# Message sums over edges: one float32 product against two float32r products of a rounded part and the rest

## The reference, cut to what matters

```python
hs = xs @ w_in2f_s / math.sqrt(B)
hv = jnp.einsum('nbc,bf->nfc', xv, w_in2f_v) / math.sqrt(B)
s = hs[idx_j]
v = hv[idx_j]
...
edge = jnp.concatenate([(t_s1 * Wf[..., 0])[..., None], (t_s2 * Wf[..., 1])[..., None],
                        t_v1 * Wf[..., 2:3], t_v2 * Wf[..., 3:4], ...], axis=-1)
agg = jax.ops.segment_sum(edge.reshape(edge.shape[0], -1), idx_i, num_segments=n).reshape(n, F, 16)
s_in = jnp.concatenate([agg[..., 0], agg[..., 1]], axis=1)
v_in = jnp.concatenate([agg[..., 2:5], agg[..., 5:8]], axis=1)
```

## Time and profile before

| | |
|---|---|
| median of 3 runs | 2253.58 us (2251.02 to 2253.9) |
| the profiled execution, own time | 2249.59 us |
| its span | 2247.9 us |
| mean granted clock of PE | 0.991 |
| instructions in the trace | 36380 |

### The profile page before, as it was taken

The page is one execution under the profiler, slowest core; times in us unless marked ns, Lnnn a source line. Parts: engine busy times, 40 slices in busy tenths (PEclk is TensorE's granted clock), DMA queues, the critical chain, the costliest instruction groups (busy, mean ns, idle before and its releaser), DMA issues.

```text
span 2247.9 us, 36380 instructions
## 1 busy us (share of the span) xinstructions
PE 2199.6 (98%) x12269; PEld 1888.6 (84%) x12269; DVE 1487.8 (66%) x4615; ACT 1024.2 (46%) x2028; POOL 937.4 (42%) x931
## 2 busy tenths in 40 slices
PE   8999999979999999999999999999999999999997
PEld 6878878858899888888999999988888777888785
DVE  8777878744767856666326666267776777678675
ACT  5982112222366632222224656344434666676454
POOL 2017637745222234376552223013444554753542
PEclk9999999989999999999999999999999999999998
DMA  6434665443476748787225667356667777776442
GB/s 215 148 133 136 161 194 193 150 137 106 138 249 216 275 151 278 254 285 252 84 92 175 221 225 258 108 187 227 218 219 236 252 251 246 246 256 227 164 124 69
DMA packets 192495, 435.82 MB, mean 194 GB/s; under 512 B 45751, under 2 KB 74622, under 8 KB 191774
## 3 DMA queue, kind: packets, MB, share of 16 engines
q1 hardware_dynamic: 127034, 249.08, 32.2%
q0 software_dynamic: 65296, 184.67, 26.3%
HBM read 242.68 MB, written 190.96 MB: 193 GB/s over the span
## 4 chain that ended last, share of the span: by engine, by line
PE 72%; DVE 2%; DMA 1%; ACT 1%; issue 1%; POOL 0%; POOLq 0%; SPq 0%; ACTq 0%; DVEq 0%
PE g_h_ps L2625 7%; PE g_h_ps L2642 7%; PE g_h_ps L2627 7%; PE g_h_ps L2626 7%; PE g_h_ps L2643 6%; PE g_h_ps L2644 6%; PE g_h_ps L2667 6%; PE g_h_ps L2669 5%; PE g_h_ps L2668 5%; PE g_t_ps L80 4%; PE g_h_ps L1783 2%; PE g_h_ps L1785 2%; PE g_h_ps L1784 2%; PE g_sum_ps L1023 1%; PE g_sum_ps L1022 1%
## 5 line engine op out<-in xcount | busy, mean ns | idle before, releaser
L2764 ACT ACTIVATE g_act_t<-g_t_ps,g_b_col 128x256 f32<-128x256 f32 (+1 forms) x488 | 202.0, 466 | 371.9 <-PE g_t_ps L80 371.7
L2642 PE MATMUL g_h_ps<-g_x_hi,held_w_hi 128*128 128x256 f32 x1216 | 352.5, 290 | 0.0
L2643 PE MATMUL g_h_ps<-g_x_lo,held_w_hi 128*128 128x256 f32 x1216 | 344.2, 283 | 0.0
L2644 PE MATMUL g_h_ps<-g_x_hi,held_w_lo 128*128 128x256 f32 x1216 | 344.1, 283 | 0.0
L632 DVE CUSTOM_DVE_ANT_0 g_prod<-g_h_sb,g_a_rows 128x256 f32<-128x256 f32 x632 | 224.3, 419 | 79.7 <-ACT g_h_sb L513 71.9
L2667 PE MATMUL g_h_ps<-fc_w_hi,g_x_hi 128*128 128x512 f32 x632 | 268.8, 425 | 2.1 <-DVE g_x_lo L2943 2.1
L2625 PE MATMUL g_h_ps<-held_w_hi,g_x_hi 128*128 128x512 f32 x656 | 264.0, 402 | 0.0
L2627 PE MATMUL g_h_ps<-held_w_hi,g_x_lo 128*128 128x512 f32 x656 | 257.2, 392 | 0.0
L2626 PE MATMUL g_h_ps<-held_w_lo,g_x_hi 128*128 128x512 f32 x656 | 257.1, 392 | 0.0
L2669 PE MATMUL g_h_ps<-fc_w_hi,g_x_lo 128*128 128x512 f32 x632 | 247.5, 392 | 0.0
L2668 PE MATMUL g_h_ps<-fc_w_lo,g_x_hi 128*128 128x512 f32 x632 | 247.0, 391 | 0.0
(11 more groups left out here) (401 smaller groups left out, 4834.2 us busy)
## 6 DMA issues: line engine op xcount, KB each, us to landing
h<-g_h_sb SPq DMA_DIRECT2D x120, 512.0 KB, 3.6
h<-g_rows_own SPq DMA_DIRECT2D x40, 512.0 KB, 4.8
g_x_in<-in_dram SPq DMA_DIRECT2D x39, 512.0 KB, 3.9
h_cols<-g_h_sb SPq DMA_DIRECT2D x38, 512.0 KB, 4.9
xb_rows<-in_dram SPq DMA_DIRECT2D x19, 1024.0 KB, 6.1
xb<-xb_rows SPq DMA_DIRECT2D x19, 1024.0 KB, 4.4
g_x_in<-h_cols SPq DMA_DIRECT2D x38, 512.0 KB, 7.6
g_x_in<-h SPq DMA_DIRECT2D x21, 512.0 KB, 6.4
```

Source lines behind the costliest of these rows:

```text
L2642: pe.matmul(out, wh, xh, start=(k == 0), stop=False)
L2643: pe.matmul(out, wh, xl, start=False, stop=False)
L2644: last = pe.matmul(out, wl, xh, start=False, stop=(k == KC - 1))
```

## The change

`sum_edges` no longer makes one float32 product. ACT copies the messages into `msg_hi`, held in float32r, right behind the carry (`carry`, now also called for tile 0, where it makes the copy alone). DVE gets a function `rest`, first in part 1, that forms `msg_lo` = `pmsg` - `msg_hi`. PE makes two products with the same mask, `msg_hi` and `msg_lo`, into one sum. The count of `msg_done` is 4 per tile instead of 3; PE waits for all 4, the others for the first 3 as before.

```diff
+    MSG_STEPS = 4
...
-                pool.wait_ge(self.msg_done, 3 * (t - 3))
+                pool.wait_ge(self.msg_done, self.MSG_STEPS * (t - 4) + 3)
...
     def sum_edges(self, pe, t):
         h = self.hold
         pe.wait_ge(self.masks_done, t + 1)
-        pe.wait_ge(self.msg_done, 3 * t + 3)
+        pe.wait_ge(self.msg_done, self.MSG_STEPS * t + 4)
         if t:
 
-            pe.wait_ge(self.carried, t)
             pe.wait_ge(self.sums_out, t)
-        pe.matmul(h.psum_ps, h.mask[:, t * P:(t + 1) * P].bitcast(F32), h.pmsg[:, :], start=True, stop=True).then_inc(self.summed, 1)
+        mask = h.mask[:, t * P:(t + 1) * P]
+        pe.matmul(h.psum_ps, mask, h.msg_hi[:, :], start=True, stop=False)
+        pe.matmul(h.psum_ps, mask, h.msg_lo[:, :], start=False, stop=True).then_inc(self.summed, 1)
...
-            act.wait_ge(self.msg_done, 3 * t)
+            act.wait_ge(self.msg_done, self.MSG_STEPS * (t - 1) + 3)
...
     def carry(self, act, t):
 
         h = self.hold
-        act.wait_ge(self.msg_done, 3 * t + 3)
-        act.activation(h.pmsg[0:1, :], h.psum_ps[0:1, :], ACT.Copy).then_inc(self.carried, 1)
+        act.wait_ge(self.msg_done, self.MSG_STEPS * t + 3)
+        if t:
+            act.activation(h.pmsg[0:1, :], h.psum_ps[0:1, :], ACT.Copy).then_inc(self.carried, 1)
+            act.wait_ge(self.carried, 2 * t)
+        act.activation(h.msg_hi[:, :], h.pmsg[:, :], ACT.Copy).then_inc(self.carried, 1)
...
+    def rest(self, dve, t):
+        h = self.hold
+        dve.wait_ge(self.carried, 2 * t + 1)
+        dve.tensor_tensor(h.msg_lo[:, :], h.pmsg[:, :], h.msg_hi[:, :].bitcast(F32), ALU.subtract).then_inc(self.msg_done, 1)
...
+        p.msg_hi, p.msg_lo = mid("msg_hi", [P, 10 * F], F32R), mid("msg_lo", [P, 10 * F], F32R)
...
-                        if 0 < n + 1 < ET:
+                        if 0 <= n + 1 < ET:
                             painn.carry(act, n + 1)
...
                     if part == 1:
+                        if 0 <= n + 1 < ET:
+                            painn.rest(dve, n + 1)
                         if 0 <= n - 2 < ET:
                             painn.add(dve, n - 2)
```

## The result

| | before | after |
|---|---|---|
| median | 2252.3 us (4 runs, 2250.44 to 2253.9) | 2270.02 us (4 runs, 2268.39 to 2272.79) |
| ratio of the times | | 1.0081, 95% interval 1.0067 to 1.0095 |
| span of the profiled execution | 2247.9 us | 2268.0 us |
| mean granted clock of PE | 0.991 | 0.988 |

The change makes the kernel 17.7 us slower.

What follows compares the result with a forecast made beforehand. PE was taken to bound the kernel. Waits of 11.7 + 3.7 + 0.85 - 0.4 = 15.9 us less 5.0 saved gave 10.9 us slower, 2264.5 us on the median; range 2254 to 2271.

Steps and rivals of the forecast that it cites:

- What bounds, and where the loss arises: PE bounds the stretch; it waits for the rest, which stands behind DVE's node-layer work, in 11 tiles, 11.7 us.
- The range: Predicted times for the whole kernel from 2254 to 2271 us, around a forecast of 2264.5 us.
- C: Rival at the edge sum on PE: two float32r products cost as much as one float32 product, 2269.5 us; 8%.
- D: Rival: ACT and DVE queues push into eight even tiles too, 6.9 us more, 2271.4 us; 12%.
- The waits: PE's waits ahead of msg_hi's product in tile 0 and the odd tiles, 15.9 us net with ACT's share and second-order terms.
- ACT's push on the shift: The copy ahead of the root on ACT delays DVE's shift 0.46 us in eight odd tiles, 3.7 us.
- The wait for the transfer: PE's existing 0.39 us wait in tile 1, which a later PE no longer sees: -0.4 us.
- Paid anew each time: DVE's lateness recurs in each odd tile, since the even tile's add between waits for PE's product.
- B: Rival: PE's wait is paid once, only the longest counting, 2.6 us in tile 19; 2251.2 us; 10%.
- The saving: Two float32r products replace PE's float32 edge sum, 0.29 us for 0.54, saving 0.25 us per tile, 5.0 us.
- rule on weight loads: Loads overlap running products only for another row group, about 107 ns each; by it 0.04 us saved per tile.
- so a late product delays them one for one: Node-layer products behind the edge sum on PE start later by exactly the wait's length, with nothing extra.

## Why the prediction was right, and where it fell short

- **What bounds, and where the loss arises**: right. PE is the bound, and PE waits in tile 0 and in the odd tiles for a rest that stands behind the node layer's work. A version that moves only that instruction takes the loss away, and so does one that leaves it out.
- **The range**: in part luck. 2270.02 us is 5.5 above the forecast of 2264.5 and 1 below the top of the range. The range reached so high for C (2269.5) and a part of D (2271.4), and the forecast's own spread ended at 2270; neither C nor D took place, and the loss of clock had no part in it. The time by itself would have spoken for C or D. Only the steps of the tiles tell them apart.
- **The waits**: right in the nine odd tiles from 3 on, a little small. The forecast steps of the nine odd tiles from 3 to 19 sum to 12.3 us, measured 13.6 (table), each 0.03 to 0.23 us more. The signal from DVE to PE takes 0.09 us, not 0.05; the copy takes 0.47 us, not 0.44; ACT's push on the shift is (8.7 - 4.7) / 8 = 0.50 us, not 0.46. Tile 8 was called tight and wasn't (-0.30 us for a forecast of -0.11). Tile 1 had a wait that the forecast lacked: the rest on DVE ended at 1925.68 us there and PE's product started at 1925.78, after 0.40 us of idle time. The wait for the transfer was gone, as forecast, so that the step came out at -0.21 us, not -0.65.
- **Paid anew each time**: right. Every odd tile waits in both profiles of the changed kernel, so B falls; no even tile but tile 0 waits, so D falls.
- **The saving**: its size was right, 0.26 us per tile by the even steps against 0.25, 5.3 us in all; its parts were not. These are tile 14 before and, without a wait, tile 14 of the changed kernel:

```profile
2014.58 0.49 PE L1534 MATMUL g_h_ps<-painn_o2s,painn_scal 128*128 128x128 f32 x2
2014.91 0.70 PE L1496 MATMUL g_sum_ps<-painn_msg,g_mask 128*128 128x320 f32 x2
...
2015.68 0.40 PE L2668 MATMUL g_h_ps<-fc_w_lo,g_x_hi 128*128 128x512 f32 x1
...
2028.63 0.49 PE L1536 MATMUL g_h_ps<-painn_o2s,painn_scal 128*128 128x128 f32 x2
2028.87 0.39 PE L1497 MATMUL g_sum_ps<-painn_msg_hi,g_mask 128*128 128x320 f32 x1
2029.10 0.30 PE L1498 MATMUL g_sum_ps<-painn_msg_lo,g_mask 128*128 128x320 f32 x1
2029.25 0.39 PE L2678 MATMUL g_h_ps<-fc_w_hi,g_x_hi 128*128 128x512 f32 x1
2029.47 0.40 PE L2679 MATMUL g_h_ps<-fc_w_lo,g_x_hi 128*128 128x512 f32 x1
```

  From the last product of `out_two` to the second one of the node layer it is 1.10 us before and 0.84 with the change. But the two products start 0.23 us apart, not 0.15, and take 0.38 us together, not 0.29. The other 0.09 us is won ahead of them, where the product starts 0.24 us behind `out_two`'s last one and not 0.33; why is not shown. That the sum came out to 0.01 us is luck in this part. The Trainium skill's rule on weight loads (TensorE: Matmul & The Clock Gate, The mechanism), by which an estimated 0.04 us would have been left, is not borne out: 0.26 us were saved, and the node product with new weights starts 0.15 us behind the second product. A part of a weight load may show in the 0.23 us between the two; no run separates it.
- **The step that failed**: "so a late product delays them one for one", said of the node layer's products behind the sum. It delays them by more. The sum counted idle time of PE at its length and had no term for PE's clock, though the stretches of 1.00 in the earlier trace rows were those of a PE that never stood. The two losses in the first profile are 2.98 + 0.26 and 1.38 + 0.26, together 4.9 us; filling the waits gives 6.2 us back between the medians. The loss of clock belonged in the forecast as a term or a rival. The Trainium skill describes on the page TensorE: Matmul & The Clock Gate (HAM oscillation — how this bites in real kernels) a kernel whose products wait for transfers, about 3 to 5 us each time, and then run at the lower clock. The traces here agree that products behind a wait can run at 1.2 GHz; they show it behind shorter waits, 0.86 to 2.55 us, and not behind each.
- **The sum** by measured parts: 13.6 for the odd steps; -2.1 for tile 1 and the seven even steps without a loss; 4.4 for tiles 6 and 16; about 1.4 for tile 0 (1.42 idle, 0.2 in the modelled end of the record ahead of it, less the saving). That is some 17 us, against 17.7 between the medians. The agreement is not as close as it looks: these parts are of one profiled execution each, which lie 20.2 us apart (2249.59 and 2269.81), and of the 4.0 us by which tile 0 starts later some 2.7 lie ahead of its wait and have no explanation here.

## What to carry to other kernels

When a change makes the bounding engine wait for something it did not wait for before, the price of the new instruction is not the question; its place in its engine's order is. Lay the timelines side by side and compare, per tile, when the bound arrives with when the other engine reaches that place: here this gave the waits of the odd tiles from 3 on to 0.23 us, and DVE's idle time in part 0, where the rest costs nothing that can be measured, stands in the same rows. Then add a term for the clock: PE's waits inside dense work cost about another third of themselves in the changed kernel's profile (4.9 us for 15.3 us idle), and over half of themselves with the copy behind the root (6.4 for 11.7).

## What the runs showed of the hardware that was not expected

- Waits of PE of 0.4 to 2.5 us, some 15 us apart, were followed by 1.2 GHz in some places and not in others: at tiles 5 and 15 in one profile of the changed kernel (6.7 and 3.3 us), at 13 and 19 in the other. With the copy behind the root it came behind waits of 0.86 and 1.40 us, while 1.70 us in tile 13 had none behind it.
- Useless products of 128x384 in PE's waits (up to 15 at a time, 12 of them in 2.36 us) went with a clock of 1.00 through the whole stretch and made the kernel 6 us faster.
- A wait of PE for DVE is shown as "issue" in 10 of 11 places here; only the run without the rest made sure of what it was.
